# Transposes of 128x128 blocks done as two 64-row halves, in long groups, with PSUM banks given out anew

## The reference, cut to what matters

```
# layer 0: 8 heads of 64, softmax of q over features and of k over positions
xn = ln(x);  q = softmax((xn@Wq+bq) per head, over d);  k = softmax(xn@Wk+bk+mask, over n)
v = (xn@Wv+bv)*mask
att = einsum('bnhd,bnhl->bhdl', k, v);  y = einsum('bnhd,bhdl->bnhl', q, att)
h = ln(y)*(1+scale)+shift;  x = x + silu(h)@W_out + b_out
# layer 1: 16 heads of 32, the usual attention
q, k, v = projections of ln(x)
p = softmax(q k^T + mask, over m);  y = p v
h = ln(y)*(1+scale)+shift;  out = x + silu(h)@out_w + out_b
```

## Time and profile before

| | us |
|---|---|
| median of 3 runs | 2092.11 (2091.98 to 2093.65) |
| the profiled execution | 2092.2 |
| its span, first to last instruction | 2090.3 |
| PE busy (matmuls) | 2065.4, 99% of the span |
| PEld busy | 1818.4, 87% |
| DVE busy | 1396.2, 67% |
| ACT busy | 1151.3, 55% |
| POOL busy | 579.0, 28% |

### The profile page before, as it was taken

The page is one execution under the profiler, slowest core; times in us unless marked ns, Lnnn a source line. Parts: engine busy times, 40 slices in busy tenths (PEclk is TensorE's granted clock), DMA queues, the critical chain, the costliest instruction groups (busy, mean ns, idle before and its releaser), DMA issues.

```text
span 2090.3 us, 48294 instructions
## 1 busy us (share of the span) xinstructions
PE 2065.4 (99%) x17499; PEld 1818.4 (87%) x17499; DVE 1396.2 (67%) x2995; ACT 1151.3 (55%) x3806; POOL 579.0 (28%) x861
## 2 busy tenths in 40 slices
PE   7999999999999999999999999999999999999997
PEld 5888888888888888888898989898898989898986
DVE  6877777777777777776665556665565655566655
ACT  4333333334323433354677777777777777777775
POOL 4323332333233322334222222222222222222220
PEclk9999999999999999999999999999999999999999
DMA  7211011100011001102210101101010101011000
GB/s 234 93 40 40 25 35 40 40 30 35 35 40 38 27 35 40 40 26 77 67 36 25 35 25 35 40 20 40 25 35 25 35 25 35 25 35 40 20 31 21
DMA packets 52165, 86.43 MB, mean 41 GB/s; under 512 B 5668, under 2 KB 14566, under 8 KB 52135
## 3 DMA queue, kind: packets, MB, share of 16 engines
q1 hardware_dynamic: 52118, 86.03, 12.1%
q10 hardware_dynamic: 16, 0.00, 0.0%
HBM read 52.32 MB, written 33.69 MB: 41 GB/s over the span
## 4 chain that ended last, share of the span: by engine, by line
PE 96%; DVE 2%; ACT 1%; DMA 0%; issue 0%; SPq 0%; POOL 0%; POOLq 0%; DVEq 0%; ACTq 0%
PE bank L538 14%; PE bank L539 14%; PE bank L540 14%; PE bank L547 9%; PE bank L548 9%; PE bank L549 9%; PE bank L1742 5%; PE bank L1755 3%; PE bank L1732 3%; PE bank L1129 3%; PE bank L1117 2%; PE bank L1014 1%; PE bank L1038 1%; PE bank L1692 1%; PE bank L1764 1%; PE bank L1042 1%
## 5 line engine op out<-in xcount | busy, mean ns | idle before, releaser
L547 PE MATMUL bank<-xT_hi,w_hi 128*128 128x256 f32 x1536 | 448.0, 292 | 0.8 <-DVE xT_lo L379 0.8
L548 PE MATMUL bank<-xT_lo,w_hi 128*128 128x256 f32 x1536 | 438.8, 286 | 0.0
L549 PE MATMUL bank<-xT_hi,w_lo 128*128 128x256 f32 x1536 | 436.1, 284 | 0.0
L1561 ACT ACTIVATE heads<-bank,top 128x128 f32<-128x128 f32 x1024 | 358.6, 404 | 88.1 <-DVE top L1354 87.9
L538 PE MATMUL bank<-w_hi,xT_hi 128*128 128x512 f32 x768 | 305.4, 398 | 0.4 <-DVE bias_all L396 0.4
L540 PE MATMUL bank<-w_lo,xT_hi 128*128 128x512 f32 x768 | 301.2, 392 | 0.0
L539 PE MATMUL bank<-w_hi,xT_lo 128*128 128x512 f32 x768 | 300.2, 391 | 0.0
L547 PEld LDWEIGHTS bank<-xT_hi,w_hi 128*128 128x128 f32 x1536 | 292.2, 190 | 8.6 <-issue 3.8
L548 PEld LDWEIGHTS bank<-xT_lo,w_hi 128*128 128x128 f32 x1536 | 292.4, 190 | 0.5 <-issue 0.5
L549 PEld LDWEIGHTS bank<-xT_hi,w_lo 128*128 128x128 f32 x1536 | 292.8, 191 | 0.0
L1354 DVE TENSOR_REDUCE top<-bank 128x4 f32<-128x512 f32 x256 | 162.8, 678 | 180.9 <-PE bank L1732 180.9
(11 more groups left out here) (203 smaller groups left out, 4048.6 us busy)
## 6 DMA issues: line engine op xcount, KB each, us to landing
xr<-in_x SPq DMA_DIRECT2D x32, 512.0 KB, 3.4
x_between_layers<-ends SPq DMA_DIRECT2D x64, 256.0 KB, 2.0
xr<-x_between_layers SPq DMA_DIRECT2D x32, 512.0 KB, 4.1
out<-ends SPq DMA_DIRECT2D x64, 256.0 KB, 2.1
store<-in_L_cond_W_emb SPq DMA_DIRECT2D x4, 1024.0 KB, 11.8
store<-in_L_cond_emb_w SPq DMA_DIRECT2D x3, 1024.0 KB, 8.0
mask_rows<-mask_parts SPq DMA_DIRECT2D x128, 2.0 KB
heads<-in_L_cond_Wk SPq DMA_DIRECT2D x1, 1024.0 KB, 7.6
```

What stands on the lines that cost most here:

```text
L547: yield nc.tensor.matmul(dst, w_hi[:, m, c, fs], a_hi[:, c], start=(first and c == 0), stop=False)
L548: yield nc.tensor.matmul(dst, w_hi[:, m, c, fs], a_lo[:, c], start=False, stop=False)
L549: yield nc.tensor.matmul(dst, w_lo[:, m, c, fs], a_hi[:, c], start=False, stop=(last and c == C - 1))
L1561: last = nc.scalar.activation(prob[:, a, c, :], ps[a][:, c * P:(c + 1) * P], ACT.Exp, bias=top[:, b, h:h + 1], accum_out=total[:, b, h:h + 1])
```

## The change

The new function `turn_halves` transposes each 128x128 block by two instructions: rows 0 to 63 in the upper half of the array, rows 64 to 127 in the lower (`tile_position` 0 and 64). Each takes 64 rows x 128 columns as the stationary operand and streams a 64-column identity. The results of the upper halves of 8 blocks fill one bank, those of the lower halves another. So every copy out of PSUM, on ACT and DVE, is now of the same half of 8 blocks instead of 4 whole blocks, with the same number of elements.

It is used in layer 0 for x, keys and queries (24 blocks in a pair), and in layer 1 for the probabilities and x (40 in a pair), except for the first pair's x of layer 1, and all probabilities of the last pair. z and yT are transposed as before. The transposes are gathered: in layer 0 keys, queries and x stand in one group after the values; in layer 1 all 16 blocks of probabilities of batch 0 and the 8 of x stand in one group between the values of batch 0 and of batch 1. Since a group needs two banks for each 8 blocks, the banks are given out anew, and the waits are set for the new owners.

```diff
+def turn_halves(nc, ident, banks, blocks):
+
+
+    half = P // 2
+    for n, src in enumerate(blocks):
+        for r in range(2):
+            rows = slice(half * r, half * r + half)
+            last = nc.tensor.transpose(banks[r][:, half * n:half * n + half], src[rows, :], ident[rows, rows],
+                                       tile_position=(half * r, 0))
+    return last
...
-    A_BANKS = (6, 2)
+    HALF = P // 2
+    A_BANKS, O_BANKS, Y_BANKS = (6, 2), (4, 0), ((5, 1), (6, 7))
+    X_BANKS, KEY_BANKS, QUERY_BANKS = (2, 3), (6, 7), (0, 1)
...
+                end_silus(i - 1)
             values(i, 0)
             values(i, 1)
+            key_rows(i)
             if not last:
-                x_low(i + 1, (ps[2], ps[3]))
+                x_low(i + 1)
             else:
                 next(following)
             if first:
-                emb.copy_rows(dve, ps[0])
+                emb.copy_rows(dve, ps[O_BANKS[0]])
             else:
-                end_add(i - 1, (i - 1) % RING, 0, 0)
-            key_rows(i, 0)
-            key_rows(i, 1)
+                end_add(i - 1, (i - 1) % RING, 0, O_BANKS[0])
             weights_of(i)
             if first:
-                emb.leave_bank(dve, ps[1])
+                emb.leave_bank(dve, ps[O_BANKS[1]])
             else:
-                end_add(i - 1, (i - 1) % RING, 1, 1)
+                end_add(i - 1, (i - 1) % RING, 1, O_BANKS[1])
             outputs(i)
             if first:
                 emb.gains(dve)
...
+        def keys_turned():
+            banks = [ps[n] for n in KEY_BANKS]
+            turn_halves(nc, ident, banks, [k_exp[:, c, b, :] for b in range(PAIR) for c in range(C)])\
+                .then_inc(s["k_tr"], 1)
+
+        def queries_turned():
+            banks = [ps[n] for n in QUERY_BANKS]
+            turn_halves(nc, ident, banks, [q_exp[:, b, c * P:(c + 1) * P] for b in range(PAIR) for c in range(C)])\
+                .then_inc(s["q_tr"], 1)
...
-            for b in range(PAIR):
-                run(project_rows(nc, w_hi, w_lo, V, xT_hi, xT_lo, b, ps[4 + b], C)).then_inc(s["v_ps"], 1)
+            run(project_rows(nc, w_hi, w_lo, V, xT_hi, xT_lo, 0, ps[4], C)).then_inc(s["v_ps"], 1)
+            value_steps = project_rows(nc, w_hi, w_lo, V, xT_hi, xT_lo, 1, ps[5], C)
+            run(islice(value_steps, 3 * C - 1))
             pe.wait_ge(s["k_exp"], seq(2, i, 2))
-            pe.wait_ge(s["q_less"], seq(PAIR, i, PAIR))
+            pe.wait_ge(s["q_exp"], seq(PAIR, i, PAIR))
+            if not first:
+                pe.wait_ge(s["g"], seq(PAIR, i - 1, PAIR))
             if not last:
-
-                x_transposed(i + 1)
+                pe.wait_ge(s["xn"], seq(PAIR, i + 1, PAIR))
+            run(value_steps).then_inc(s["v_ps"], 1)
+            keys_turned()
+            queries_turned()
+            if not last:
+                x_turned()
             else:
                 next(following)
+            pe.wait_ge(s["v"], seq(PAIR, i, PAIR))
             if first:
-                run(emb.products(pe, ps[0]))
+                run(emb.products(pe, ps[O_BANKS[0]]))
             else:
-                run(out_rows(i - 1, 0, 0))
-            weights_turned(i, 0)
-            weights_turned(i, 1)
-            outputs1 = () if first else out_rows(i - 1, 1, 1)
-            run(islice(outputs1, 7))
-
+                run(out_rows(i - 1, 0, O_BANKS[0]))
+
+            pe.wait_ge(s["k_rows"], seq(2, i, 2))
...
         return vcol("L1_cond_norm_w", c)
 
-    Y_BANK, Z_BANK, O_BANK = 4, 7, 6
-    QK_BANKS, V_BANKS, X_BANKS = (5, 6), (5, 6), (5, 7)
+    Z_BANK, EMB_BANK = 4, 4
+    Y_BANKS, O_BANKS = (5, 7), (6, 4)
+    QK_BANKS, V_BANKS, X_BANKS = (7, 6), (5, 5), (7, 6)
+    HALF = P // 2
     FIRST_QK_BANKS, FIRST_V_BANKS = ((0, 1), (2, 3)), (4, 6)
...
+        def x_high(pair, r):
+            if r == 0:
+                act.wait_ge(s["v_ps"], seq(PAIR, pair - 1, PAIR))
+            act.wait_ge(s["xT_ps"], seq(PAIR, pair, PAIR))
+            nc.scalar.activation(xT_hi[:, :, :, HALF * r:HALF * r + HALF],
+                                 ps[X_BANKS[r]][:, :].rearrange("p (c b t) -> p c b t", c=C, b=PAIR),
                                  ACT.Copy).then_inc(s["xT_hi"], 1)
 
...
+        def prob_turned():
+
+            for a in (0, 2):
+                turn_halves(nc, ident, (ps[a], ps[a + 1]), [prob[:, a + n, c, :] for n in range(2) for c in range(C)])\
+                    .then_inc(s["pT_ps"], 2)
+
...
             run(value_rows(i, 0))
-            z_transposed(i - 1, 1)
-            prob_turned(i, 0, (0, 1))
+            z_turned = z_transposed(i - 1, 1)
+            run(islice(z_turned, C - 1))
+            pe.wait_ge(s["prob"], seq(PAIR * C, i, C))
+            pe.wait_ge(s["xn"], seq(PAIR, i + 1, PAIR))
+            pe.wait_ge(s["y"], seq(PAIR, i - 1, PAIR))
             pe.wait_ge(s["out"], seq(PAIR, i - 1, 1))
+            run(z_turned)
+            prob_turned()
+            x_turned()
+            pe.wait_ge(s["v"], seq(PAIR, i, 1))
             run(value_rows(i, 1))
-            prob_turned(i, 0, (2, 3))
-            pe.wait_ge(s["v"], seq(PAIR, i, 1))
-            x_transposed(i + 1, 0)
             pe.wait_ge(s["g"], seq(PAIR, i - 1, PAIR))
-            x_transposed(i + 1, 1)
-            pe.wait_ge(s["v"], seq(PAIR, i, PAIR))
             run(out_rows(i - 1, 1))
-            mixed(i, 0, False)
+            mixed(i, 0, Y_BANKS[0])
...
             run(projected(i + 1, K, (2, 3)))
             if first:
                 pe.wait_ge(emb.s["scale"], 1)
-            z_transposed(i, 0)
+            else:
+                pe.wait_ge(s["out"], seq(PAIR, i - 1, PAIR))
+            run(z_transposed(i, 0))
+            pe.wait_ge(s["prob"], seq(PAIR * C, i, PAIR * C))
             pe.wait_ge(s["k"], seq(2, i + 1, 1))
             run(projected(i + 1, Q, (0, 1)))
-            prob_turned(i, 1, range(HC))
+            prob_turned()
             pe.wait_ge(s["k"], seq(2, i + 1, 2))
             run(projected(i + 1, Q, (2, 3)))
-            mixed(i, 1, first)
+            pe.wait_ge(s["q"], seq(2, i + 1, 1))
+            mixed(i, 1, Y_BANKS[1])
 
```

Copies out of PSUM follow the halves; this one stands for them all (`x_low`, `key_rows` and `query_T` in layer 0, `x_low`, `x_high` and `prob_out` in layer 1):

```diff
         def prob_out(i, b, some):
             for a in some:
                 act.wait_ge(s["pT_ps"], seq(PAIR * C, i, b * C + a + 1))
+                first, r = a // 2 * 2, a % 2
+                nc.scalar.activation(prob_T[:, first:first + 2, :, HALF * r:HALF * r + HALF],
+                                     ps[a][:, :].rearrange("p (n c t) -> p n c t", n=2, c=C),
+                                     ACT.Copy).then_inc(s["pT"], 1)
```

More of the change, by code:

```diff
@@ L818, in values, with key_rows @@
                                            ALU.mult, ALU.add).then_inc(s["v"], 1)
[L820 to L823, removed]
+        def key_rows(i):
+            dve.wait_ge(s["k_tr"], seq(1, i, 1))
+            for r in range(2):
+                nc.vector.tensor_copy(k_rows[:, :, :, HALF * r:HALF * r + HALF],
+                                      ps[KEY_BANKS[r]][:, :].rearrange("p (b c t) -> p b c t", b=PAIR, c=C))\
+                    .then_inc(s["k_rows"], 1)
         def weights_of(i):
@@ L921, in _, with x_high @@
     def _(act):
[L922 to L925, removed]
+        def x_high(pair):
+            act.wait_ge(s["xT_ps"], seq(PAIR, pair, PAIR))
+            for r in range(2):
+                nc.scalar.activation(xT_hi[:, :, :, HALF * r:HALF * r + HALF],
+                                     ps[X_BANKS[r]][:, :].rearrange("p (c b t) -> p c b t", c=C, b=PAIR),
                                      ACT.Copy).then_inc(s["xT_hi"], 1)
@@ L1007, in _, with x_turned @@
         following = second["tensor"](pe)
-        def x_transposed(pair):
-            for b in range(PAIR):
-                pe.wait_ge(s["xn"], seq(PAIR, pair, b + 1))
-                for c in range(C):
-                    last = nc.tensor.transpose(ps[2 + b][:, c * P:(c + 1) * P], xn[:, b, c * P:(c + 1) * P], ident[:])
-                last.then_inc(s["xT_ps"], 1)
+        def x_turned():
+            banks = [ps[n] for n in X_BANKS]
+            turn_halves(nc, ident, banks, [xn[:, b, c * P:(c + 1) * P] for c in range(C) for b in range(PAIR)])\
+                .then_inc(s["xT_ps"], PAIR)
         def z_transposed(prev):
@@ L1070, in body @@
                     continue
-                if f == 2:
+                if f == 0:
                     pe.wait_ge(emb.s["scale"], 1)
+                if f == 2 and not first:
+                    pe.wait_ge(s["y"], seq(PAIR, i - 1, 1))
                 keys(f)
@@ L1192, in v_banks @@
     def v_banks(pair):
-        if isinstance(pair, int) and pair in (0, LAST):
-            return LAST_V_BANKS if pair else FIRST_V_BANKS
-        return V_BANKS
+        return FIRST_V_BANKS if isinstance(pair, int) and pair == 0 else V_BANKS
     def sync(sp):
@@ L1487, in vector @@
         for b in range(PAIR):
-            x_low(0, b, (2, 3))
+            first_x_low(b, 2 + b)
         yield
```

(8 more changed lines are left out.)

158 lines of the change are left out of this document (85 added, 73 removed).

## The result

The changed kernel takes 2085.4 us (median of 10 runs, 2085.0 to 2087.4), the one before 2092.05 (10 runs, 2091.8 to 2094.1): a ratio of 0.9967, 95% interval 0.9958 to 0.9977. That is 6.7 us faster; the prediction had said 15.4.

A forecast was written before the change was run, and what follows sets the result against it. PE bounds the kernel, busy for 2065.4 of 2090.3 us. Layer 0's -31.9 and -0.5, layer 1's +18.0 and its first pair's -1.05 make -15.4: from 2092.2 to 2076.8 us, range 2055 to 2100.

The forecast's parts named there:

- +1.08 - 0.48 = +0.60: Layer 1's loop, us a pair: step0 loses 1.08, step1's group of 16 gains 0.48; 30 pairs +18.0.
- The block, 0.060: PE, each block turned by halves: 0.060 us instead of 0.109, bounds 0.0545 to 0.069; 2000 blocks in all.
- the forecast's 0.069: Pitch in us of a 64-row transpose alone in its half, slow first one included; upper bound for a block.
- The rival that loads bind: Halves barely overlap or 128-column loads set the pitch: 0.106 or 0.138 us a block, 2169 or 2233 us; 11 in 100.
- In and out of the split array, 0.31: PE, each of 94 groups by halves: changing mode in and out costs 0.31 us.
- Layer 0, -1.03 a pair, no new wait: Layer 0's transposes: 2.78 us a pair becomes 1.75, everything ready in time; 31 pairs give 31.9 less.
- I take 0.06 from the signal to its start ... 0.20: Layer 1, step0: last z transpose waits for all 16 exponentials, 0.14 us late plus 0.06 for a load without overlap.
- The pause for h_lo, 1.70: Layer 1, step0: PE stands 1.70 us before batch 1's output rows, in each of 30 pairs.
- the chain of 1.93: Layer 1, step0: 1.93 us from the last values matmul through DVE's `values` and `low_part` to batch 1's output rows.
- the third rival: PE's clock falls in the new pauses, 1 us lost in each of 30 pairs: +30, 2107 us; 3 in 100.
- The first pair, 1.05: Layer 1's first pair, without output rows in step0, gains 1.05 us, including 0.48 from step1.

The follow-up runs named there:

- runs of four: Changed kernel with four upper row halves turned, then four lower ones, and so on in each group: 2090.81 us, ratio 0.9985.
- runs of eight: Changed kernel with all upper row halves of each group queued before all lower ones: 2130.88 us, ratio 1.0185.

## Why the prediction was off

It named the right direction, mechanism and places. The step that failed is the size of the one on layer 1, "+1.08 - 0.48 = +0.60": the traces show +1.33 - 0.42 in one pair and 0.92 a pair over all of them. Two terms in it were too small, the late start behind the signal for prob (0.35 instead of 0.20) and the price of a group by halves. The result is a small difference of two large amounts, some 33 us gained and 18 lost in the forecast, so 0.3 a pair was enough to turn 15.4 into 6.7. Step by step:

- **The block, 0.060.** 0.0622 measured: the column halves of the earlier trace rows gave 0.030 an instruction, the row halves have 0.031. Two thousand blocks make 4 us of it. The transposes of the earlier trace rows had the better figure: in their single records the pitch is 0.062 behind the slow first one, and the forecast's 0.069 has that one in it. The rival that loads bind is out. The Trainium skill, TensorE: Matmul & The Clock Gate, LDWEIGHTS (loading the stationary operand), would have given 107 ns for a load of 128 columns; the measurement differs: two of them, one in each half, fit into every 62 ns.
- **In and out of the split array, 0.31.** 0.35: the runs by group (1.84 for 24, 1.33 for 16, 0.84 for 8) and the run with one more group a pair (+11 of 31 x 0.35) agree; the 94 groups make 4 us of the difference. The two terms together made a group of 24 cost 1.84 instead of 1.75, one of 16 some 1.33 instead of 1.27. In a pair of layer 1 that is 0.09 in step0 and 0.06 in step1, 5 us in all.
- **Layer 0, -1.03 a pair, no new wait.** The group cost 0.09 more, and the order gave 0.09 back between y and the keys, which I had not seen; at layer 1's first z transpose the kernel was 34.0 ahead against 33.0. Of this 1.0, some 0.4 is already there at layer 0's first z transpose (62.55 and 62.17 in the single records). That the sum for layer 0 came out is in part luck: two errors of 0.09 cancel. No wait recurs, as said.
- **"I take 0.06 from the signal to its start ... 0.20" (step0's new wait).** This term failed by most in a pair. The half blocks start 0.35 late, not 0.20: from the end of ACT's last read to the last z transpose it is 0.25, not 0.06. Three more waits stand behind the one for prob, all met by then, and PE works them off only after prob has come; with them out of the way it is 0.06, the start is 0.19 late, the forecast's figure, and 4.0 us come back. I had priced the signal and not the queue behind it.
- **The pause for h_lo, 1.70, and the chain of 1.93.** The chain is 1.93, its wait by the profile 1.53, since the profile counts a single matmul as busy for 0.39 and not for its pitch of 0.23: the distance is what matters. The last matmul of the values moved by what start and group add: 0.35 + 1.84 - 0.87 = 1.32 of the 1.33.
- **The clock.** With the 30 pauses the granted clock is 1.00 from 1020 to 1500 us and 0.99 from 1500 to 2080, the same as before; up to 2060 it is 1.00 in both kernels, so the fall lies in the last stretch, as in the earlier trace rows. No sign of the third rival.
- **The first pair, 1.05.** Its step1 gained 0.1 instead of 0.48 (the next z transposes stand 34.1 ahead). PE waits there once, for 0.24, for a copy of the probabilities (ACT, L1606) ahead of `mixed`; the forecast had no such wait.

Sum of the misses in layer 1: 0.15 (start) + 0.09 + 0.06 = 0.30 a pair, 9.0 us, and 0.4 in its first pair; the 1.0 further ahead at its start goes against them. That leaves 8.4 of the 8.7 between forecast and result. Left open: the 0.09 between y and the keys. A version with the waits directly at the half blocks, instead of at a whole transpose ahead of them, wasn't tried.

## What to carry to other kernels

Before speeding up a group of instructions, ask what its length was covering: here 58 us of saved PE work came out as 7, because the group moved from behind to ahead of the matmul that starts a 1.93 us chain over another engine. The same group put between that matmul and the chain's end, with the values as cover for the wait for prob, brings all of it, 69 us. And of several waits in a row, those that are met long before belong somewhere earlier, and only the late one stands last.

## What the runs showed of the hardware

Row halves of the array overlap fully: 64 x 128 loads with 64 streamed fp32 columns start 3 to 4 ns apart, a pair every 62.2 ns (109 for a whole block). They need not stand strictly by turns: runs of four cost one pitch more a group, runs of eight a quarter more a block (0.076). In these the ninth instruction, for the free half, starts with the fifth, ahead of three others, which I read as a look some three places past one that its half can't take yet; what sets this reach no run tells. Entering and leaving this mode costs 0.35 us a group, so eight blocks by halves (0.84) are hardly cheaper than whole (0.87). The Trainium skill, TensorEngine Tiling (Array Packing), Key Properties, says that tiles load and multiply in parallel and that a change of mode drains the array. The first agrees with the starts 3 to 4 ns apart; the second fits the 0.35 us, though no run here shows what that time is spent on. Three waits that are already met cost PE 0.13 to 0.16 us when they stand behind one that isn't.
